# A routed expert kernel on one core: both scatter-adds of a pair under way, and the last stored rows ahead of later weights

## What is computed

```python
x = x + tanh(g_xattn[0]) * xattn(layernorm(x), ctx, ctx, lens, lens, W, b)
logits = layernorm(x) @ router_w.T            # 8 experts
routing = softmax(logits)
top_w, top_i = top_k(routing, 2)
top_w = top_w / sum(top_w)
g = einsum('nd,ehd->neh', xf, w_gate)
u = einsum('nd,ehd->neh', xf, w_up)
y = einsum('neh,edh->ned', silu(g) * u, w_down)
x = x + tanh(g_ffn[0]) * einsum('ned,ne->nd', y, combine)
```

## Time and profile before

| | |
|---|---|
| time, median of 3 runs | 436.59 us (436.02 to 437.37) |
| profiled execution | 439.98 us, span 438.2 us |
| TensorE busy | 414.4 us, 95% of the span |
| VectorE busy | 313.4 us, 72% |
| ScalarE busy | 282.3 us, 64% |
| POOL busy | 258.4 us, 59%, of which adds 119.4 (68 of them) and gathers 94.1 (76) |
| moved | 50.52 MB, 115 GB/s over the span |

### The profile page before, as it was taken

One profiled execution on the slowest core, in us unless ns is written; L12 is line 12 of the kernel. 1 busy time (PEld: TensorE's weight loads), 2 busy tenths in 40 slices (PEclk: granted clock), 3 DMA queues, 4 the chain that ended last, 5 costly groups with the idle time before them and its releaser, 6 DMA issues.

```text
span 438.2 us, 9841 instructions
## 1 busy us (share of the span) xinstructions
PE 414.4 (95%) x3249; PEld 378.4 (86%) x3249; DVE 313.4 (72%) x691; ACT 282.3 (64%) x569; POOL 258.4 (59%) x271
## 2 busy tenths in 40 slices
PE   8999999985899998999999999999999999999991
PEld 3777766542899998999999999999999999999991
DVE  6567999882567676767668777777776877777771
ACT  2577786403477675777676776767767677676770
POOL 7005646625256556667667665676667666567664
PEclk9999999997999999999999999999999999999997
DMA  6956776786357665343334343333433334333343
GB/s 198 326 187 199 253 232 226 237 263 210 110 137 178 153 160 123 51 65 55 54 68 61 61 63 59 50 59 61 63 59 52 58 61 66 56 51 58 62 63 65
DMA packets 34720, 50.52 MB, mean 115 GB/s; under 512 B 3878, under 2 KB 26055, under 8 KB 34695
## 3 DMA queue, kind: packets, MB, share of 16 engines
q0 software_dynamic: 13536, 19.46, 27.1%
q1 hardware_dynamic: 19815, 29.84, 21.8%
q10 hardware_dynamic: 1344, 0.92, 0.7%
HBM read 32.51 MB, written 17.70 MB: 115 GB/s over the span
## 4 chain that ended last, share of the span: by engine, by line
PE 62%; DMA 16%; issue 7%; DVE 5%; POOL 4%; ACT 4%; SPq 1%; POOLq 0%; ACTq 0%; DVEq 0%
PE Y L1241 18%; PE GT L1220 17%; PE UP L1220 16%; DMA out_rows<-y,idx 7%; PE XT L1211 3%; PE S L1095 3%; DMA xt<-xn_rows,idx 3%; DMA xTg<-in_xT 3%; DMA xn_rows<-pay 2%; POOL xt L499 2%; PE O L1144 1%; ACT ex L590 1%; POOL out_rows L507 1%; DVE xg L874 1%; DMA raw<-in_weights 1%
## 5 line engine op out<-in xcount | busy, mean ns | idle before, releaser
L507 POOL DMA_INDIRECT out_rows<-y,idx x68 | 119.4, 1755 | 97.0 <-ACT y L661 54.1
L1013 DVE TENSOR_TENSOR gu<-raw,gu 128x1024 fp32r<-128x1024 f32 x70 | 85.8, 1225 | 65.3 <-ACT gu L637 62.0
L1220 PE MATMUL GT<-xtT,gu 128*128 128x256 f32 x828 | 114.4, 288 | 1.2 <-ACT hid L650 1.1
L499 POOL DMA_INDIRECT xt<-xn_rows,idx x76 | 94.1, 1239 | 34.0 <-issue 33.4
L1220 PE MATMUL UP<-xtT,gu 128*128 128x256 f32 x828 | 110.6, 283 | 0.0
L1220 PEld LDWEIGHTS GT<-xtT,gu 128*128 128x128 f32 x828 | 104.7, 192 | 2.9 <-ACT hid L650 1.4
L1220 PEld LDWEIGHTS UP<-xtT,gu 128*128 128x128 f32 x828 | 104.3, 192 | 0.0
L1241 PE MATMUL Y<-dn,hT 128*128 128x256 f32 x816 | 103.5, 283 | 0.0
L1241 PEld LDWEIGHTS Y<-dn,hT 128*128 128x128 f32 x816 | 100.4, 192 | 0.0
L637 ACT CAST gu<-raw 128x1024 fp32r x68 | 70.8, 1042 | 34.3 <-PE UP L1220 32.8
L1034 DVE TENSOR_TENSOR hid<-hid,UP 128x512 f32<-128x512 f32 x68 | 46.5, 683 | 9.5 <-PE UP L1220 9.5
(11 more groups left out here) (165 smaller groups left out, 392.4 us busy)
## 6 DMA issues: line engine op xcount, KB each, us to landing
raw<-in_weights SPq DMA_DIRECT2D x32, 384.0 KB
xn_rows<-pay SPq DMA_DIRECT2D x8, 528.0 KB, 3.5
xTg<-in_xT SPq DMA_DIRECT2D x8, 512.0 KB, 4.0
xg<-in_x SPq DMA_DIRECT2D x8, 512.0 KB, 6.0
out_rows<-xg SPq DMA_DIRECT2D x8, 512.0 KB, 3.9
xt<-xn_rows,idx POOLq DMA_INDIRECT x76
out_rows<-y,idx POOLq DMA_INDIRECT x68
kr<-in_ctx_rows SPq DMA_DIRECT2D x1, 308.0 KB
```

The costliest lines, as they stand in the source:

```text
L499: gp.indirect_dma_start(out=xt[:, 2 * s + t, :], out_offset=None, in_=xn_rows, in_offset=bass.IndirectOffsetOnAxis(ap=idx[:, 2 * j + t:2 * ...
L507: gp.indirect_dma_start(out=out, out_offset=bass.IndirectOffsetOnAxis(ap=idx[:, 2 * j + t:2 * j + t + 1], axis=0), in_=y[:, j % 2, t, :], ...
L1013: return tt(out=out, in0=whole, in1=high.bitcast(F32), op=ALU.subtract)
L1220: last = mm(bank[:, h * PT:(h + 1) * PT], gu[:, pw, q, c, w, h * P:(h + 1) * P], xtT[:, b, px, c], start=(c == 0 and n == 0), stop=(c == D ...
```

## The change

In SP's program the store of the last group's rows moves ahead of expert 2's weights. Expert 2's weights now wait for the gathers of pairs 0 and 1, experts 4 to 7 for those of pairs 2 and 3 as before.

In POOL's program each pair's work is now: add tile 0, add tile 1, gather both tiles of pair j+4, read a number. Tile 0's add waits for both adds of all pairs before. Tile 1's waits for a number read from a new table `adds_due`: the same count as tile 0's, or 16 more (so for tile 0's add too) where the list says that tile 1 is empty. An empty tile's rows are all padding rows, which tile 0 also names where it is not full. The number is read (`value_load`) from SBUF behind the pair before. VectorE makes the table with three small instructions. ScalarE's wait before it writes y is for both adds of the pair two before, for either tile.

```diff
@@ SP @@
-            load_weights(2, range(PARTS))
-            store_xn(GROUPS - 1)
-            load_weights(3, range(PARTS))
-            for s in range(AHEAD):
-
+            store_xn(GROUPS - 1)
+
+            sp.wait_ge(tile_loaded[0], 32)
+            sp.wait_ge(tile_loaded[1], 32)
+            load_weights(2, range(PARTS))
+            load_weights(3, range(PARTS))
+            for s in range(2, AHEAD):
                 sp.wait_ge(tile_loaded[s], 32)
@@ POOL @@
-            def add(j, t):
-
-                pool.wait_ge(y_added, 16 * (2 * j + t) + Y_ADDED0)
+            def add(j, t, adds_before=None):
+
                 pool.wait_ge(y_ready, 2 * j + t + 1 + Y_READY0)
+                if t == 0:
+                    pool.wait_ge(y_added, 32 * j + Y_ADDED0)
+                else:
+
+                    pool.wait_ge(y_added, adds_before)
...
+            pool.wait_ge(tables_ready, 1)
+
+            def added_before(j):
+                return pool.value_load(adds_due[0:1, j:j + 1], min_val=Y_ADDED0, max_val=32 * PAIRS + Y_ADDED0)
+
+            def pair_out(j, due):
+                add(j, 0)
+                add(j, 1, due)
+
+                if j + AHEAD < PAIRS:
+                    for t in range(2):
+                        gather(j + AHEAD, t)
+
+            due = added_before(0)
             for j in range(LEAST):
-                for t in range(2):
-                    add(j, t)
-
-                    gather(j + AHEAD, t)
+                pair_out(j, due)
+                due = added_before(j + 1)
@@ ScalarE @@
-                    act.wait_ge(y_added, 32 * j + 16 * t - 48 + Y_ADDED0)
+                    act.wait_ge(y_added, 32 * j - 32 + Y_ADDED0)
@@ VectorE @@
+            empty = mark(ts(second_empty[:], L[0:1, LIST:LIST + TILES].rearrange("p (j t) -> p j t", t=2)[:, :, 1], 0.0, 16.0,
+                            ALU.is_equal, ALU.mult))
...
+            after(empty)
+            due = mark(stt(out=due_J[:], in0=J[:], scalar=16.0, in1=second_empty[:], op0=ALU.mult, op1=ALU.add))
             ts(pairs_used[:], cum[0:1, NE - 1:NE], 0.5, None, ALU.mult)
+
+            after(due)
+            ts(adds_due[:], due_J[:], float(Y_ADDED0), None, ALU.add)
```

More of the change, by code:

```diff
@@ L73, in moe_flamingo @@
         pairs_used = sb("pairs_used", [1, 1], I32)
+        adds_due = sb("adds_due", [1, PAIRS], I32)
         pad_tile = sb("pad_tile", [P, ROW])
@@ L167, in moe_flamingo @@
         tex = sb("tex", [1, PAIRS], F32, a)
+        second_empty = sb("second_empty", [1, PAIRS], F32, a)
+        due_J = sb("due_J", [1, PAIRS], F32, a)
         xg = sb("xg", [P, XS * G, D], F32, a)
@@ L520, in _, with rest @@
                     gather(j, t)
+            pool.wait_ge(tables_ready, 1)
[8 more added lines that the diff above has]
+            due = added_before(0)
             for j in range(LEAST):
-                for t in range(2):
-                    add(j, t)
-                    gather(j + AHEAD, t)
+                pair_out(j, due)
+                due = added_before(j + 1)
             used = pool.value_load(pairs_used[:], min_val=LEAST, max_val=PAIRS)
-            def rest(j):
+            def rest(j, due):
                 if j < PAIRS:
                     with pool.If(used > j):
[L531 to L537, removed]
+                        pair_out(j, due)
+                        rest(j + 1, added_before(j + 1) if j + 1 < PAIRS else None)
+            rest(LEAST, due)
         @block.scalar
```

## The result

The changed kernel takes 429.93 us (median of 6 runs, 429.77 to 430.38); the kernel before takes 436.6 in 6 runs beside it. The ratio is 0.9844, with a 95% interval of 0.9824 to 0.9864: faster by 6.7 us, where 9.7 were forecast. Some executions of either kernel take 1.5% or more longer than its fastest, and medians and ratios here leave those out. The profiled execution took 430.38, with a span of 428.6. Against the profiled execution of before (439.98 and 438.2) that is 9.6 less, almost the forecast sum. The two comparisons differ by 2.9 us, and most of the experiments are about that difference.

A forecast was written before the change was run, and what follows sets the result against it. TensorE was taken as the bound, with transfers setting the time at the hand-over, in the weight stretch and in the tail. 5.0 + 3.3 + 1.4 = 9.7 us off the 436.59 median gives 426.9; range 425.0 to 430.6.

The forecast's parts named there:

- the forecast itself: Whole kernel: the central range of 425.0 to 428.5 us, given chance 0.62.
- a low clock: Rival at the hand-over to the experts: TensorE's clock falls anyway; 428.5 to 430.6 us, chance 0.12 together with a late store.
- a late store: Rival at the hand-over: group 7's store lands at 99.8, leaving 1.3 to 2.9 us; chance 0.12 together with a low clock.
- adds that gain nothing in the middle: Rival in the pair loop: count always asks, or transfers stretch each other; 430.2 us, with the tail 431.6; full chance unstated.
- SP's order: Hand-over from attention to experts: earlier store gains 3.38 on the gather, 0.47 on transposes, 1.16 on gates; 5.0 us.
- Two adds under way, the middle: 33 down-projection steps: second add no longer held by the first's landing, POOL doesn't fall behind; 3.3 us gained.
- The tail: After the last down-projection: last gather starts earlier and, not the add, limits the end; 1.0 to 1.7, taken as 1.4 us.
- POOL's time: POOL's work per pair: 7.52 to 8.41 us, with the count's read 7.8 to 8.7, hidden in its wait for y.
- The weights: Weights 2 and 3 start some 14 us later, but casts come later still: nothing waits, 0 us.
- The rival of the other side: POOL becomes the bound through the count's load behind each pair's gathers; 441.8 us, chance 0.07.
- The rival that the count always asks: One cause of the middle rival: the table's count always asks for the first add; 430.2 us, with the tail 431.6.

The follow-up runs named there:

- The lone experiment: Kernel before with only SP's new order: last group's store ahead of expert 2's weights, these waiting for gathers of pairs 0 and 1; 430.99 us, ratio 0.9899.
- the adds' part alone: Changed kernel with SP's order put back as before, so only the adds' new order remains; 435.72 us, ratio 0.9978 to the kernel before.
- the eighth experiment: Changed kernel without the gathers of pairs 32 and 33, which nothing uses; 428.35 us, ratio 0.9805 to the kernel before.
- the fifth experiment: Changed kernel with the table's count always asking for the first add, so no two adds of a pair are under way; 471.28 us, ratio 1.0731.
- the tenth experiment: Kernel before with SP's new order and without gathers that no pair uses, adds in the old order; 430.46 us, ratio 0.9866.

## Why the prediction was right, and where it was off

**The time: right in part by luck.** 429.93 lies inside 425.0 to 430.6, but above the 425.0 to 428.5 that were the forecast itself. That part of the range was kept for rivals, above all for a low clock, a late store or adds that gain nothing in the middle (426.9 + 3.3 = 430.2). Clock and store came as forecast, and the adds did what they should; the time still came out beside that last rival's, because the median had hardly any stall to lose. The time alone could not have told these two apart; the waits in the profiles do.

**SP's order: right, 5.5 instead of 5.0.** From index to first down-projection it was 22.38 (120.09 less 97.71) before and 16.58 (114.58 less 98.00) after, 5.8 less; the index itself came 0.3 later. The forecast's parts: the gather followed the last release by 1.07 before and by 0.29 now, where 1.07 was kept (0.8 more gained). The landing was 2.77 instead of 3.11 (0.3 more). The clock stayed, and transposes and gates gave 0.5 and 1.1, as forecast. Afterwards 0.3 went back, between the first up-projection and the first down-projection. The lone experiment gives 6.0 us by the medians and 4.4 by the ratio, most of the change either way. The store's place alone gives 4.6 by the medians (436.97 less 432.33); holding the weights back is worth 0.2 to 0.5 at the start in the profiles, and by their ratios the two are not told apart. The 1.1 of the gates has the weakness of the next term: it is read from one execution, and in five in which the clock had fallen they took 1.97 to 3.12.

**Two adds under way, the middle: mechanism right, size wrong.** The step that failed is "so POOL doesn't fall behind, and the 3.29 goes: 3.3", carried to the median with "the same 9.7 applied there gives 426.9". The stall goes, and the profiles bear the 3.2. But three profiles of the kernel before have steps of 304.22, 301.33 and 302.26, against 301.06 and 300.89 after: the stall is 3.2, 0.3 or 1.2, depending on how far POOL's adds lag in that execution. The profiled execution was 3.4 over its median, and I had that number in hand. Most of it was in all likelihood this very stall: the second profile, 2.3 shorter, has 2.9 less of it; no run shows the stall of an execution without a profile. A gain read from a part of the profile that is peculiar to it can't be subtracted from a median that doesn't have it. Taken as the remainder, 6.7 less 5.5 and 0.9, the middle gave the median 0.3; the adds' part alone gives 1.3 by the medians, of which the tail's 0.9 leave 0.4. The runs differ in their spread too: the eleven of the changed kernel lie within 0.8 us, the six with SP's order alone over 6.4. That fits adds that no longer lag, but no long run of SP's order alone was profiled.

**The tail: 0.9 instead of 1.4.** From the first y of the last pair to the last gather's start it is 6.19 (424.88 less 418.69) instead of 7.14. The first add starts 0.50 after y instead of 1.05, near the early end of what was forecast, but takes 2.17 instead of 1.60, so it ends 2.67 after y where it had ended 2.65 after. The earlier start was worth nothing: the add now starts inside a VectorE instruction that holds it (last section). What is left is the 1.0 of the new order, the low end of the forecast. The gather's landing did limit the end, as the eighth experiment shows.

**POOL's time: right, by another route.** Without a read the cycle is 8.03, inside the 7.52 to 8.41 forecast for it. Most adds are stretched to 2.4, where 1.85 and 2.49 were priced (the mean of all 68 is 2.26); the gathers take 1.0 each. The reads cost nothing, not because POOL waits for y, but because POOL's queue runs ahead and reads during the adds. The rival of the other side, POOL as the bound through its reads, is refuted even with four reads.

**The weights: wrong in a detail that costs nothing.** I wrote that nothing waits. ScalarE's casts did wait for weights in the changed kernel, four times and at most 1.4 us (once for 0.9 before, twice and up to 1.4 in the second profile of before):

```profile
ACT gu L655 <- DMA raw<-in_weights: 3.8, 4, 1.4
```

None of it reached TensorE: its steps are at the full pace, and its waits hold neither a gate nor an up-projection that lacked weights.

**The rival that the count always asks** is real as a mechanism but was priced far too low: 471.28, not 430.2 or 431.6. I had left the old order's numbers in it. In the changed kernel the count asks once, at pair 15, as worked out from the inputs (POOL's timeline):

```profile
254.55 2.40 POOL L516 DMA_INDIRECT out_rows<-y,idx  x1 [1.32 <-ACT y L679]
260.04 1.58 POOL L516 DMA_INDIRECT out_rows<-y,idx  x1 [3.08 <-DMA out_rows<-y,idx]
```

## What to carry to other kernels

Before a gain is read from one profile, compare that execution with the median: if it is longer, find where, and don't count a removal of that part in full. Look in a queue for a transfer that the next stage needs and that stands behind ones it doesn't need yet; moving it, and holding the others back, was worth 4.4 to 6.0 of 6.7 us here, most of it by the move. An order of instructions and its waits are one thing: with a gather between two adds the wait for a landing is mostly hidden, with the adds side by side it must go.

## What the hardware showed beyond that

An add's time on POOL depends on where VectorE stands. From the timeline of the changed kernel:

```profile
409.59 1.22 DVE L1038 TENSOR_TENSOR dn<-raw,dn 128x1024 fp32r<-128x1024 f32 x1
409.90 2.40 POOL L516 DMA_INDIRECT out_rows<-y,idx  x1 [2.17 <-ACT y L679]
...
412.41 1.23 DVE L1038 TENSOR_TENSOR gu<-raw,gu 128x1024 fp32r<-128x1024 f32 x1 [0.57 <-ACT gu L655]
412.60 2.49 POOL L516 DMA_INDIRECT out_rows<-y,idx  x1 [0.30 <-issue]
```

Both adds start inside a VectorE instruction with two inputs in SBUF, and both end 1.5 us after its end (412.30 less 410.81, and 415.09 less 413.64). So do all 57 adds of this trace that start inside such an instruction, within 0.1 us. One that starts outside takes 1.58 to 1.62, also when the instruction begins while it runs. In the kernel before, 18 adds start inside a VectorE instruction that has one input in PSUM (`xtT` and `hid`), and they take 1.59 to 1.61: these don't hold an add. The Trainium skill (SBUF — State Buffer, Who interferes with whom) says that a VectorE instruction with two inputs in SBUF and a GpSimd one that reads SBUF exclude each other, and the rows agree.

A landing is mostly seen earlier with another transfer of POOL's behind it. From the end of an add's instruction to the start of the add that waits for it, it is 2.4 to 2.6 in pairs 12 to 31 of the kernel before, with a gather between, and 2.9 to 3.2 in all 34 pairs of the fifth experiment, with none; pair 15 of the changed kernel has 3.1. Longer ones occur either way: 3.8 with a gather between while weights stream, 4.0 without at the end of the tenth experiment. What causes it stays open; no run here isolates it.
